# Routing per image with rows scattered to expert lists, and experts started on three images' full blocks while the last image is normed and routed

## The chip, the cores and the metric

The kernel runs on one core of a Trainium2 chip. The metric is the device time of one launch in microseconds (us). PE is TensorE, PEld its weight loads, DVE VectorE, ACT ScalarE, POOL GpSimd, SP SyncE, which here only issues DMAs. A name with a q behind it (SPq) is an engine's instruction queue.

## The reference

Four images of 256 channels x 1024 pixels go through group norm and a full attention over pixels, a second attention on layer-normed tokens, and a mixture of experts. The last part is what the change is about:

```
t = t + _L1_attn_ref(_ln_t(t), ...)
t = t + _L1_ffn_ref(_ln_t(t), ...)
# _L1_ffn_ref, 4096 tokens of 256 numbers, 8 experts, 1024 hidden units:
x_norm = _layernorm(x, ln_g, ln_b)
xf = x_norm.reshape(B * S, D)
probs = jax.nn.softmax(xf @ gate_w, axis=-1)
dispatch_w, expert_idx = jax.lax.top_k(probs, TOP_K)        # TOP_K = 2
combine = jnp.sum(jax.nn.one_hot(expert_idx, E) * dispatch_w[..., None], axis=1)
for e in range(E):
    h = jax.nn.gelu(xf @ w1[e] + b1[e], approximate=False)
    out = out + combine[:, e:e + 1] * (h @ w2[e] + b2[e])
return x + out
```

For the inputs of the reference, experts 0 to 7 are chosen 471, 363, 1370, 373, 1459, 939, 273 and 2944 times; in the first three images 371, 263, 1011, 276, 1133, 680, 215 and 2195 times.

## The kernel before, in words

Every float32 product is made of three passes (`three`) over a rounded half and a remainder of each operand; ACT makes the rounded half (a cast), DVE the remainder (a subtraction). All engines run hand-written programs that meet at semaphores.

**Images.** `image(b, first, last)` runs on each engine for b = 0 to 3. Its first part is the pixel attention, its second the group R of 24 projections (`for gi, ... in enumerate(R)`), its third the second attention: eight turns of `scores` and `mix2` on PE. The norms of image b-1, the transposes of its normed rows (`gate_turn`) and its gate products (`gate`, logits to `gate_read`) are woven into image b. Those of image 3 stand behind it, on their own. SP writes the stream (`acc_rows`) and the normed rows (`xf_rows`) of each image to memory.

**Routing.** After image 3 and after a meeting of all engines (`ends(..., 1, ...)`), `route` on DVE finds each token's two experts, its place in its expert's list, and with 64 matmuls on one-hot matrices (`pick_lo`, `pick_hi`) the tables `gather_at`, `scatter_at` and `slot_w`. Lists are padded to blocks of 256 rows.

**Expert steps.** A step s is one block of one expert; experts come in ascending order, and with the counts above there are 2, 2, 6, 2, 6, 4, 2 and 12 blocks, 36 steps. Steps run in pairs (i, n), s = 2i + n, in a loop. In a step, PE makes for f = 0 to 7 a first product (hidden columns 128f to 128f+127) and a second product, with first products three f ahead (`AHEAD = 3`), and at f = 1 it transposes the rows of step s+1 (`x_turn`). ACT makes the gelu of each first product into one of four slots `h32`, DVE splits it into `hs`; second product f waits for that (`h_lo`). At f = 3 ACT scales the output of step s-1 (`y_scale`, into `y_w`, semaphore `y_act`), and POOL adds it to the stream with two indirect DMAs (`scatter`, semaphore `added`). POOL also gathers the rows of step s+2 with two indirect DMAs (`gather`).

**Weights.** A step's raw weights (w1 and w2 of an expert, 1 MB each) are loaded by SP (`expert_load`) into buffer n = s mod 2, and split in eight pieces of 512 columns by ACT (`w_piece`) and DVE. Split weights have two buffers too (`w1s[n]`, `w2s[n]`), so step s compares its expert with that of step s-2 (`fresh`); if it is the same one, nothing is loaded or split. Here that makes 16 loads. The pieces of step s+1 are made during step s, at ACT's f = 0 to 7.

**End.** SP waits for the last scatter, loads the stream, PE transposes it, and SP stores the output.

Of the kernel before, what the change touches and what calls it, by code (L numbers as in the profile page):

```python
# [29 lines left out]
P = 128  # L30
ALU = mybir.AluOpType
# [19 lines left out]
def hybrid_block_kernel(nc, x, q_w, k_w, v_w, oT, q_b, v_b, out_b, gn, W1, W2T, a_qk, a_vT, Wout,  # L51
# [15 lines left out]
    COLS = STEPS * SUB  # L67
# [3 lines left out]
    assert KC == 2 and STEPS % 2 == 0 and NT == 8 and NH == 2 and TILES * E == 256  # L71
# [4 lines left out]
    xf_d = nc.dram_tensor("xf_rows", (TOK, C), F32, kind="Internal").ap()  # L76
    acc_t = acc_d.rearrange("(t p) c -> p t c", p=P)
    xf_t = xf_d.rearrange("(t p) c -> p t c", p=P)
# [4 lines left out]
    with ctx:  # L83
# [18 lines left out]
        logits = sb("logits", [P, TILES, E])  # L102
        top8 = sb("top8", [P, TILES, 8])
        top_i = sb("top_i", [P, TILES, 8], mybir.dt.uint32)
# [15 lines left out]
        bs("to_224", [P, 56])  # L120
        pr = [bs(f"pr{i}", [P, 2, T], F32R) for i in range(2)]
        bs("to_0", [P, 8])
        xf = bs("xf", [P, NT, C])
# [4 lines left out]
        xfT = sb("xfT", [P, KC, T], F32, here)  # L128
        here.close()
# [10 lines left out]
        x2 = sb("x2", [P, NT, C], F32, here)  # L140
# [7 lines left out]
        sb("to_32", [P, 8], F32, here)  # L148
# [4 lines left out]
        minus_one = bs("minus_one", [P, 8])  # L153
# [24 lines left out]

        tl_bn = bs("tl_bn", [P, 2, NT, 6])
        tl_mv = bs("tl_mv", [P, 2, NT, 2])  # L180
        tl_eps = bs("tl_eps", [P, 2, NT])
        tl_r = bs("tl_r", [P, 2, NT])
        tl_mr = bs("tl_mr", [P, 2, NT])
        tl_nb = bs("tl_nb", [P, 2, NT])
        batch_scope.close()


        route_scope = ExitStack()

        def rs(name, shape, dt=F32):  # L190
            return sb(name, shape, dt, route_scope)

        expert_of = ctx.enter_context(nc.sbuf_tensor("expert_of", [P, STEPS], I32))

        fresh = ctx.enter_context(nc.sbuf_tensor("fresh", [P, STEPS + 2], I32))
        live = sb("live", [P, PAIRS], I32)
        last_step = sb("last_step", [P, 1], I32)
        gather_at = sb("gather_at", [P, COLS + 2 * SUB], I32)
        scatter_at = sb("scatter_at", [P, COLS], I32)
        slot_w = sb("slot_w", [P, COLS])  # L200
        before = rs("before", [P, P])
        iota_i = rs("iota_i", [P, P], I32)
        iota = rs("iota", [P, P])
        top_f = rs("top_f", [P, 2, TILES])
        exps = rs("exps", [P, TILES, E])
        zsum = rs("zsum", [P, TILES])
        zinv = rs("zinv", [P, TILES])
        is_top = rs("is_top", [P, 2, TILES, E])
        either = rs("either", [P, TILES, E])
        scratch = rs("scratch", [P, 2, TILES, E])  # L210
        top_w = rs("top_w", [P, 2, TILES])
        prefix = [rs(f"prefix{i}", [P, TILES, E]) for i in range(2)]
        slot_all = rs("slot_all", [P, TILES, E])
        cnt_f = rs("cnt_f", [P, E])
        cnt_i = rs("cnt_i", [P, E], I32)
        cnt_s = rs("cnt_s", [P, E], I32)
        need = rs("need", [P, E])
        ends_t = [rs(f"ends{i}", [P, E]) for i in range(2)]
        base = rs("base", [P, E])
        past = rs("past", [P, STEPS, E])  # L220
        expert_f = rs("expert_f", [P, STEPS])
        other = rs("other", [P, STEPS])
        end_i = rs("end_i", [P, 1], I32)
        slot_f = rs("slot_f", [P, 2, TILES])
        slot_i = rs("slot_i", [P, 2, TILES], I32)
        lo_i = rs("lo_i", [P, 2, TILES], I32)
        hi_i = rs("hi_i", [P, 2, TILES], I32)
        lo_f = rs("lo_f", [P, 2, TILES])
        hi_f = rs("hi_f", [P, 2, TILES])
        number_i = rs("number_i", [P, TILES], I32)  # L230
        number = rs("number", [P, TILES])
        PICK = 8
        pick_lo = rs("pick_lo", [P, 2 * TILES, P])
        pick_hi = rs("pick_hi", [P, 2 * TILES, 2, COLS])
        one_hot = rs("one_hot", [P, 2 * TILES, COLS])
        at_f = rs("at_f", [P, COLS])
        at_m = rs("at_m", [P, COLS])
        route_scope.close()
# [7 lines left out]
        es("to_512", [P, 16])  # L246
        xg = es("xg", [P, 2, SUB, C])
        xt = [[es(f"xt{n}{i}", [P, KC, STEP], F32R) for i in range(2)] for n in range(2)]
        h32 = es("h32", [P, 4, STEP])
        hs = [es(f"hs{i}", [P, FC, STEP], F32R) for i in range(2)]  # L250
        y_b = es("y_b", [P, SUB, C])
        y_w = es("y_w", [P, 2, SUB, C])
        es("w1_to_32", [P, 8])
        w1s1 = [es(f"w1s1{i}", [P, KC, FF], F32R) for i in range(2)]
        es("w2_to_192", [P, 40])
        w2s1 = [es(f"w2s1{i}", [P, FC, C], F32R) for i in range(2)]

        es("past_route", [P, 10240])
# [3 lines left out]
        es("w1_to_224", [P, 8])  # L262
        w1s = ([es(f"w1s0{i}", [P, KC, FF], F32R) for i in range(2)], w1s1)
        es("w2_to_32", [P, 16])
# [180 lines left out]
        def _(sp):  # L445
# [98 lines left out]
            with sp.Fori(1, PAIRS) as i:  # L544
                with is_live(sp, i):
                    for n in range(2):
                        expert_load(i * 2 + n, n, i, False)
# [1411 lines left out]
```

## Time and profile before

| | us |
|---|---|
| Median of 3 runs (1246.24 to 1247.96) | 1247.34 |
| The profiled execution's own time | 1251.48 |
| Its span, first to last instruction | 1249.8 |
| PE busy in it | 1149.5 |
| End of the last `mix2` to the first expert product | 93.8 |
| First expert product to the end of the last one | 431.7 |

A row of the timeline gives start, duration, engine, line, operation, out<-in, count, and in brackets the idle time of the engine before it with what ended it. Rows of one engine that follow each other closely are merged, with their count. PE's rows overlap: a row's duration is longer than its distance to the next.

### The profile page before, as it was taken

The page shows a single profiled execution, that of the slowest core. Times are in us where ns is not written, and L with a number is a line of the kernel's source. Part 1 is how long each engine was busy: PE and PEld are TensorE (multiplying, and loading weights), DVE is VectorE, ACT ScalarE, POOL GpSimd, SP SyncE. Part 2 cuts the span into 40 slices and gives each one's busy share as a digit, 9 for nine tenths or more (in the row PEclk, how much of TensorE's full clock was granted, in tenths as well). Part 3 has the DMA queues.
Part 4 walks back from the last instruction along what each step waited for, and adds up shares of the span by engine and source line. Part 5 has one row for each costly group of instructions (what it writes and reads, how often), then busy time and mean ns, then how long its engine had stood idle before and what let it go on. Part 6 is the DMA issues. An engine that isn't in the chain of part 4 may idle for free.

```text
span 1249.8 us, 25051 instructions
## 1 busy us (share of the span) xinstructions
PE 1149.5 (92%) x8118; PEld 1072.8 (86%) x8119; DVE 823.7 (66%) x1883; ACT 545.2 (44%) x995; POOL 343.2 (27%) x352
## 2 busy tenths in 40 slices
PE   6999999999999999999999334999999999999993
PEld 5898998988988989989898234999999999999992
DVE  4676475964667744778436787796796778856651
ACT  2533445432435334444333313674564556634431
POOL 0010002500004300024000325355555455555440
PEclk9999999999999999999999558899999999999996
DMA  5000000210001100011000233363573547533238
GB/s 165 1 2 33 1 1 1 69 34 1 1 2 35 68 1 1 1 35 35 1 1 1 67 114 107 101 193 54 164 207 53 145 100 215 150 59 55 55 47 273
DMA packets 66206, 82.70 MB, mean 66 GB/s; under 512 B 11104, under 2 KB 56544, under 8 KB 66144
## 3 DMA queue, kind: packets, MB, share of 16 engines
q1 hardware_dynamic: 52128, 63.48, 15.8%
q0 software_dynamic: 14016, 18.37, 8.2%
q8 instruction: 42, 0.69, 0.2%
q14 instruction: 20, 0.16, 0.0%
HBM read 60.85 MB, written 22.02 MB: 66 GB/s over the span
## 4 chain that ended last, share of the span: by engine, by line
PE 89%; DVE 6%; DMA 2%; issue 1%; SPq 1%; ACT 1%; POOL 0%; POOLq 0%; DVEq 0%; ACTq 0%
PE ps L1553 81%; PE ps L1633 2%; PE ps L1843 1%; PE ps L1595 1%; PE ps L1566 1%; DMA rows<-acc_rows 1%; DVE one_hot L1103 1%; DVE pick_hi L1111 1%; PE ps L1586 1%; PE ps L1642 1%; PE ps L1655 1%; DVE pick_lo L1106 1%; DMA o_row<-in_out_b 1%; DMA xg<-xf_rows,now_g 0%; SPq L559 0%
## 5 line engine op out<-in xcount | busy, mean ns | idle before, releaser
L1553 PE MATMUL ps<-xt,w1s 128*128 128x256 f32 x1746 | 257.5, 284 | 1.5 <-DVE xt L1484 1.5
L1553 PE MATMUL ps<-w2s,hs 128*128 128x256 f32 x1728 | 250.1, 280 | 3.3 <-issue 2.5
L1553 PEld LDWEIGHTS ps<-xt,w1s 128*128 128x128 f32 x1746 | 227.9, 190 | 2.3 <-DVE xt L1484 1.9
L1553 PEld LDWEIGHTS ps<-w2s,hs 128*128 128x128 f32 x1728 | 222.8, 188 | 4.7 <-issue 4.7
L952 ACT ACTIVATE h<-ps,b1t 128x256 f32<-128x256 f32 x288 | 137.4, 478 | 112.4 <-PE ps L1553 78.8
L712 POOL DMA_INDIRECT acc_rows<-y_w,now_s x72 | 119.9, 1666 | 165.3 <-issue 154.2
L1520 DVE CAST hs<-h 128x256 fp32r<-128x256 f32 x288 | 92.1, 320 | 70.1 <-ACT h L952 48.2
L1522 DVE TENSOR_TENSOR hs<-h,hs 128x256 fp32r<-128x256 f32 x288 | 123.0, 427 | 9.9
L1553 PE MATMUL ps<-xs,wh 128*128 128x512 f32 x384 | 121.3, 397 | 1.5 <-issue 1.5
L594 POOL TENSOR_TENSOR tl_r<-tl_eps,minus_half 128x4 f32<-128x4 f32 x16 | 16.2, 1014 | 350.0 <-DVE tl_eps L1224 350.0
L699 POOL DMA_INDIRECT xg<-xf_rows,now_g x76 | 92.8, 1222 | 47.4 <-POOL now_g L695 34.7
L1553 PE MATMUL ps<-vs,pr 128*128 128x256 f32 x768 | 97.7, 283 | 0.0
L1553 PEld LDWEIGHTS ps<-vk,pr 128*128 128x128 f32 x768 | 92.4, 188 | 3.6 <-DVE pr L1365 0.9
L1553 PE MATMUL ps<-xs,qs 128*128 128x512 f32 x384 | 95.4, 397 | 0.0
L1553 PE MATMUL ps<-vk,pr 128*128 128x256 f32 x768 | 93.1, 277 | 0.7 <-DVE pr L1365 0.7
L1553 PE MATMUL ps<-qs,ks 128*128 128x512 f32 x384 | 93.2, 393 | 0.0
L1553 PEld LDWEIGHTS ps<-vs,pr 128*128 128x128 f32 x768 | 92.0, 188 | 0.0
L1360 DVE TENSOR_REDUCE neg_max<-ps 128x1 f32<-128x1024 f32 x32 | 39.2, 1224 | 79.9 <-PE ps L1553 79.9
L1553 PEld LDWEIGHTS ps<-qs,ks 128*128 128x128 f32 x384 | 70.2, 188 | 14.0
L1553 PEld LDWEIGHTS ps<-xs,wh 128*128 128x128 f32 x384 | 69.4, 188 | 14.5 <-issue 1.7
L1553 PEld LDWEIGHTS ps<-xs,qs 128*128 128x128 f32 x384 | 69.8, 188 | 13.5
L1553 PE MATMUL ps<-xs,wl 128*128 128x512 f32 x192 | 75.0, 391 | 0.0
(213 smaller groups left out, 1874.8 us busy)
## 6 DMA issues: line engine op xcount, KB each, us to landing
w1r<-in_w SPq DMA_DIRECT2D x16, 1024.0 KB
w2r<-in_w SPq DMA_DIRECT2D x16, 1024.0 KB, 8.6
b2t<-in_b SPq DMA_DIRECT2D x36, 128.0 KB
xn<-in_x SPq DMA_DIRECT2D x4, 1024.0 KB, 4.8
acc_rows<-r_out SPq DMA_DIRECT2D x4, 1024.0 KB, 4.5
xf_rows<-xf SPq DMA_DIRECT2D x4, 1024.0 KB, 5.0
rows<-acc_rows SPq DMA_DIRECT2D x8, 512.0 KB, 7.3
out_tokens<-cols_out SPq DMA_DIRECT2D x8, 512.0 KB, 8.8
```

The lines of the kernel that those rows point to most:

```text
L594: return g.tensor_tensor(dst, src, minus_half[:, 0:src.shape[1]], ALU.pow)
L699: g.indirect_dma_start(out=xg[:, n, h, :], out_offset=None, in_=xf_d, in_offset=bass.IndirectOffsetOnAxis(ap=now_g[:, n, h:h + 1], axis=0) ...
L712: g.indirect_dma_start(out=acc_d, out_offset=bass.IndirectOffsetOnAxis(ap=now_s[:, n, h:h + 1], axis=0), in_=y_w[:, n, h, :], in_offset=No ...
L952: a.activation(h32[:, gi % 4, :], bank(gi % 4, STEP), ACT.Gelu, bias=b1t[:, n, f:f + 1]).then_inc(h_act, 1)
L1103: v.tensor_tensor(one_hot[:, j, :], iota[:, 0:COLS].unsqueeze(1).to_broadcast((P, PICK, COLS)), hi_f[:, k, t].unsqueeze(2).to_broadcast((P ...
L1106: v.tensor_tensor(pick_lo[:, j, :], iota[:, :].unsqueeze(1).to_broadcast((P, PICK, P)), lo_f[:, k, t].unsqueeze(2).to_broadcast((P, PICK, P)),
L1111: v.tensor_tensor(pick_hi[:, j, 1, :], one_hot[:, j, :], top_w[:, k, t].unsqueeze(2).to_broadcast((P, PICK, COLS)), ALU.mult).then_inc(pic ...
L1360: v.tensor_reduce(neg_max[:, i:i + 1], bank(2 * (i % 2), count=2), AXX, ALU.max, negate=True).then_inc(s2_max, 1)
L1520: v.tensor_copy(hs[0][:, f, :], h32[:, gi % 4, :]).then_inc(h_hi, 1)
L1522: v.tensor_tensor(hs[1][:, f, :], h32[:, gi % 4, :], hs[0][:, f, :].bitcast(F32), ALU.subtract).then_inc(h_lo, 1)
L1553: ins = t.matmul(out, left[l], right[r], start=first and n == 0, stop=last and n == 2, **more)
L1633: ins = t.transpose(bank(4, count=2)[:, j * P:(j + 1) * P], prob[:, i % 2, j * P:(j + 1) * P], ident[:, :])
```

## The change

The routing of an image becomes part of the work woven into the next one. In group R, DVE takes logits to two experts per token (`gate_read`, `tops`, `choose`), PE sums how many earlier tokens chose the same expert (`ranks`, ten small matmuls), DVE makes list places and weights (`slots`, `weigh`), and POOL writes each normed row, with weights and row number behind its 256 numbers, to both of its experts' lists in memory (`send_rows`, 16 indirect DMAs an image). Lists have a fixed place for each expert. `x2`, the tables of one-hot matrices and `xf_rows` are gone.

When three images are in the lists, their full blocks are 1, 1, 3, 1, 4, 2, 0 and 8; the first 12 of them are steps 0 to 11 (phase A, experts in descending order), and the rest is phase B in ascending order. With the counts above the steps' experts are 5 5 4 4 4 4 3 2 2 2 1 0 | 0 1 2 2 2 3 4 4 5 5 6 6, and 7 twelve times. The norms, gate, routing and row writes of image 3 are placed by hand at certain (s, f) of steps 0 to 8 (`on`, `..._AT`). Steps 0 to 9 are written out; the loop begins at step 10, behind nine DMAs that write empty rows to the lists' ends, and behind the last row writes.

Split weights now have one buffer (`w1s`, `w2s`); `fresh` compares step s with step s-1, which makes 13 loads: for steps 0, 2, 6, 7, 10, 11, 13, 14, 17, 18, 20, 22 and 24. Six pieces are made during the step before, from ACT's f = 1 on (`W_AT`), two during the step itself (`LATE_AT`). The rows of a step are one plain DMA by SP; they bring the row numbers and weights, which POOL copies out before SP may fill the buffer again (`note_step`, semaphore `noted`).

```diff
+    A_STEPS = 12
+    B_STEPS = STEPS - A_STEPS
+    LOOP_AT = A_STEPS // 2 - 1
...
+        RANK_AT = 21
+        RANK_BANK = 3
+        EARLY = {4: (0, 1), 5: (2, 3), 6: (4, 5), 7: (6, 7)}
+        W_PIECES = ((0, 0), (0, 1), (1, 0), (0, 2), (1, 1), (0, 3))
+        W_AT = {1: 0, 3: 1, 4: 2, 5: 3, 6: 4, 7: 5}
+        LATE_AT = {0: 2, 3: 3}
...
+        STATS_AT = {(0, 1): 0, (0, 2): 1}
+        XF_AT = {(0, 4): (0,), (0, 5): (1,), (0, 6): (2,), (0, 7): (3,), (1, 0): (4,), (1, 1): (5,), (1, 2): (6,), (1, 4): (7,)}
+        GATE_TILES_AT = {(2, 4): (0, 1), (2, 5): (2, 3), (2, 6): (4, 5), (2, 7): (6, 7)}
+        ROWS_AT = {4: (0,), 5: (1, 2), 6: (3, 4), 7: (5, 6), 8: (7,)}
```

The loads on SP:

```diff
+            def gather(s, n, first):
+                if not first:
+                    sp.wait_ge(xt_mm, at(s, 1, -1))
+                    sp.sem_inc(sp_held, 1)
+                    sp.wait_ge(noted, at(s, 2, -2))
+                    sp.sem_inc(sp_held, 1)
+                row = sp.value_load(row_of[0:1, bass.ds(s, 1)], min_val=0, max_val=PAD)
+                sp.dma_start(xg[:, n, :, :], sorted_d[bass.ds(row, STEP), :].rearrange("(h p) c -> p h c", p=P)
+                             ).then_inc(g_in[n], 16)
...
+            def expert_load(s, n, u):
+
+                sp.wait_ge(wl_act, at(s, LATE, -LATE))
+                sp.sem_inc(sp_held, 1)
+                sp.wait_ge(wl_dve, at(s, LATE, -LATE))
+                sp.sem_inc(sp_held, 1)
+                e = expert(s)
+                with sp.If(sp.value_load(fresh[0:1, bass.ds(s, 1)], min_val=0, max_val=1) == 1):
+                    weights(n, e)
...
+            def steps(i, first):
+                for n in range(2):
+                    s = i * 2 + n
+                    if not first:
+                        expert_load(s, n, i)
+                    gather(s + 2, n, False)
+                    if isinstance(i, int) and s == 3:
+                        rows_of(B - 1)
...
+            for e in range(E + 1):
+                at_row = sp.value_load(pad_at[0:1, e:e + 1], min_val=0, max_val=PAD - STEP) if e < E else PAD
+                sp.dma_start(sorted_d[bass.ds(at_row, STEP), :].rearrange("(h p) c -> p h c", p=P),
+                             pad_row[:, :].unsqueeze(1).to_broadcast((P, SUB, ROW))).then_inc(pad_in, 16)
+            sp.wait_ge(pad_in, (E + 1) * 16)
+            sp.wait_ge(rows_in, B * NT * 2 * 16)
+            with sp.Fori(LOOP_AT, PAIRS) as i:
```

POOL:

```diff
+            def send_rows(b, tiles):
+
+                pool.wait_ge(slot_done, at(b, 1, 1))
+                pool.wait_ge(weighed, at(b, 1, 1))
+                pool.sem_inc(pool_held, 1)
+                for t in tiles:
+                    for k in range(2):
+                        g.indirect_dma_start(out=sorted_d, out_offset=bass.IndirectOffsetOnAxis(
+                            ap=slot_i[:, k, t:t + 1], axis=0), in_=xf[:, t, :], in_offset=None,
+                            bounds_check=PAD - 1, oob_is_err=True).then_inc(rows_in, 16)
...
+            def note_step(s, n, u):
+
+                if not (isinstance(s, int) and s < 2):
+                    pool.wait_ge(added, at(s, SUB * 16, -SUB * 16))
+                pool.wait_ge(g_in[n], at(u, 16, 16))
                 pool.sem_inc(pool_held, 1)
...
+                e = pool.value_load(expert_of[0:1, bass.ds(s, 1)], min_val=0, max_val=E - 1)
+                g.tensor_copy(now_s[:, n, :], xg[:, n, :, NUMBER]).then_inc(noted, 1)
+                g.tensor_copy(now_w[:, n, :].unsqueeze(2),
+                              xg[:, n, :, bass.ds(e + WEIGHT, 1)]).then_inc(noted, 1)
...
+            def steps(i):
                 for n in range(2):
                     s = i * 2 + n
...
+                    if not (isinstance(i, int) and s == 0):
+                        scatter(s - 1, 1 - n, isinstance(i, int) and s == 1)
+                    note_step(s + 1, 1 - n, (i if n == 0 else i + 1))
```

ACT (the gelu lines stand as before):

```diff
+            def w_piece(s, n, u, which, p):
+
+                first = isinstance(s, int) and s == 0
+                act.wait_ge((w1_in, w2_in)[which][n], at(u, 16, 16))
+                if not first:
+                    act.wait_ge((h_mm, y_mm)[which], at(s, FC, 2 * p + 2 - FC))
...
                     a.activation(h32[:, gi % 4, :], bank(gi % 4, STEP), ACT.Gelu,
                                  bias=b1t[:, n, f:f + 1]).then_inc(h_act, 1)
...
+                    if late and f in LATE_AT:
+                        w_piece(s, n, i, 1, LATE_AT[f])
+                    if split and f in W_AT:
+                        w_piece(s + 1, 1 - n, (i if n == 0 else i + 1), *W_PIECES[W_AT[f]])
```

PE:

```diff
+            def ranks(b, at_bank, c):
+
+                pe.wait_ge(chosen, at(b, 1, 1))
+                out = bank(at_bank)
+                t.matmul(out[:, c:c + NT * E], before[:, :], either[:, :, :].rearrange("p t e -> p (t e)"),
+                         start=True, stop=False)
+                for d in range(1, NT):
+                    t.matmul(out[:, c + d * E:c + NT * E], ones[:, :],
+                             either[:, 0:NT - d, :].rearrange("p t e -> p (t e)"), start=False, stop=False)
...
-            pe.wait_ge(p2_exp, B * NT)
-            gate_turn(B - 1)
-            gate(B - 1, range(NT))
-            pe.wait_ge(g_mm, B)
-            pe.sem_inc(pe_end, 1)
```

**The order on SP.** In the loop before, the rows from one weight load's first wait to its DMAs, in the odd step of a pair. They wait for the pieces of an earlier step alone.

```order
L513 ISA [waits ws_act,ws_dve]
L513 TENSOR_LOAD expert_of
L513 ISA x2
L524 REGISTER_ALU
L524 TENSOR_LOAD fresh
L524 ISA x2
L524 COMPARE_AND_BRANCH
L516 ISA
L516 DMA w1r<-in_w 128x2x1024
L518 DMA w2r<-in_w 128x8x256
```

Now, in the written-out steps, from the rows of step s+2 to the weights of step s+1.

```order
L541 TENSOR_LOAD row_of [waits xt_mm,noted]
L541 ISA x2
L542 ISA
L542 DMA xg<-sorted_rows 128x2x272
L546 TENSOR_LOAD expert_of [waits wl_act,wl_dve]
L546 ISA x2
L555 TENSOR_LOAD fresh
L555 ISA x2
L555 COMPARE_AND_BRANCH
L517 ISA
L517 DMA w1r<-in_w 128x2x1024
L519 DMA w2r<-in_w 128x8x256
```

The load of step s+1 now stands behind a wait for `noted` of step s.

**The order on POOL.** Now, one step in the written-out part: the scatter of step s-1, then the note of step s+1.

```order
L762 DMA acc_rows<-y_w,now_s 4096x256 [waits noted,y_act]
L762 DMA acc_rows<-y_w,now_s 4096x256
L751 TENSOR_LOAD expert_of [waits added,g_in0]
L751 ISA x2
L752 CAST now_s<-xg 128x2
L753 ISA
L753 COPY now_w<-xg 128x2
```

The note waits for `added`, which the two DMAs ahead of it raise when they have landed.

**The order on ACT.** Now, in the loop, the start of a step whose successor has new weights: the second gelu, the first weight piece, the third gelu.

```order
L1049 ACTIVATE h<-ps,b1t 128x256 [waits h_lo]
L965 ISA
L967 ISA [waits w1_in0]
L970 CAST w1s<-w1r 128x2x256 [waits h_mm]
L1046 REGISTER_ALU
L1048 REGISTER_ALU [waits h_mm]
L1049 ACTIVATE h<-ps,b1t 128x256 [waits h_lo]
```

The third gelu of step s stands behind the wait for w1 of step s+1. Before, the first piece stood one gelu earlier and waited for its load in the same way.

## Rows read from the trace of the kernel before

**Rows 1.** The page's busy time of each engine.

```profile
PE 1149.5 (92%) x8118; PEld 1072.8 (86%) x8119; DVE 823.7 (66%) x1883; ACT 545.2 (44%) x995; POOL 343.2 (27%) x352
```

**Rows 2.** PE's timeline from the last mix2 to the first expert products.

```profile
684.56 5.93 PE L1553 MATMUL ps<-vk,pr 128*128 128x256 f32 x48 [0.71 <-DVE pr L1365]
...
784.29 5.01 PE L1553 MATMUL ps<-xt,w1s 128*128 128x256 f32 x24 [1.46 <-DVE xt L1484]
```

**Rows 3.** Timeline of all engines at the last step's end.

```profile
1215.11 0.87 PE L1553 MATMUL ps<-w2s,hs 128*128 128x256 f32 x6
...
1220.64 1.55 POOL L712 DMA_INDIRECT acc_rows<-y_w,now_s  x1 [0.30 <-issue]
1223.74 7.14 SPq L559 DMA_DIRECT2D rows<-acc_rows  x8
```

**Rows 4.** The chain that ended last: seven steps without new weights lie between.

```profile
1112.54 11.25 PE ps L1553 x96
...
1194.43 11.28 PE ps L1553 x96
```

**Rows 5.** Timeline of all engines in one step with new weights.

```profile
811.42 0.48 ACT L952 ACTIVATE h<-ps,b1t 128x256 f32<-128x256 f32 x1 [0.42 <-PE ps L1553]
...
813.58 0.60 PE L1843 MATMUL ps<-ident,xg 128*128 128x128 f32 x4
...
815.58 0.92 ACT L967 ACTIVATE y_w<-y_b,slot_w 128x256 f32<-128x256 f32 x2
...
816.14 0.87 PE L1553 MATMUL ps<-w2s,hs 128*128 128x256 f32 x6
...
817.90 1.62 POOL L712 DMA_INDIRECT acc_rows<-y_w,now_s  x1 [4.23 <-issue]
...
819.83 1.91 POOL L712 DMA_INDIRECT acc_rows<-y_w,now_s  x1 [0.31 <-issue]
...
820.52 0.44 DVE L1522 TENSOR_TENSOR hs<-h,hs 128x256 fp32r<-128x256 f32 x1
...
820.88 0.68 DVE L1474 TENSOR_TENSOR w2s<-w2r,w2s 128x512 fp32r<-128x512 f32 x1
```

**Rows 6.** Timeline around two weight loads: SP's issues, and ACT's first piece.

```profile
910.99 0.35 SPq L540 DMA_DIRECT2D b2t<-in_b  x1
...
914.72 0.01 SPq L516 DMA_DIRECT2D w1r<-in_w  x1
...
919.59 0.62 ACT L912 CAST w1s<-w1r 128x512 fp32r<-128x512 f32 x1 [2.67 <-DMA w1r<-in_w]
...
922.99 0.34 SPq L540 DMA_DIRECT2D b2t<-in_b  x1
925.15 0.38 SPq L516 DMA_DIRECT2D w1r<-in_w  x1
...
930.24 0.62 ACT L912 CAST w1s<-w1r 128x512 fp32r<-128x512 f32 x1 [0.91 <-DMA w1r<-in_w]
```

**Rows 7.** Windows: stretch, its length, PE busy, granted clock (1.00 full, 0.50 half), DMA.

```profile
692.00:696.00 4.00, 0.00 (x0) 0.63 0.00 0
696.00:700.00 4.00, 0.00 (x0) 0.50 0.01 2
...
786.00:788.00 2.00, 2.00 (x11) 0.50 0.30 102
788.00:790.00 2.00, 2.00 (x17) 0.86 0.00 0
```

**Rows 8.** DVE's timeline in the gap: `tail_add` and `tail_stats` for four tiles of image 3.

```profile
690.60 1.29 DVE L1208 TENSOR_TENSOR tok<-ps,tok 128x512 f32<-128x512 f32 x2 [3.97 <-PE ps L1553]
691.92 1.41 DVE L1219 BATCH_NORM_STATS2 tl_bn<-tok 128x6 f32<-128x256 f32 x4
...
693.77 0.17 DVE L1224 TENSOR_SCALAR tl_eps<-tl_mv 128x4 f32<-128x4 f32 x1
```

**Rows 9.** Timeline of PE in group R of image 2: a quarter of the gate.

```profile
448.43 0.95 PE L1595 MATMUL ps<-gate_sb,xfT 128*128 128x8 f32 x8
```

More of the change, by code:

```diff
@@ L201, in hybrid_block_kernel @@
[L201 to L224, printed above, removed]
@@ L858, in image @@
                         hi2(0)
+                    if not first and gi == RG - 4:
+                        route_exp(b - 1)
                     if gi == TN_AT - 1:
@@ L949, in chunks @@
                     act.wait_ge(h_mm, at(i, 2 * FC, gi + 1))
-                    if not (first and gi < 4):
+                    if not (new and gi < 4):
                         act.wait_ge(h_lo, at(i, 2 * FC, gi - 3))
@@ L1318, in image @@
                         max1(i + 2)
+                    if not first and i == 0:
+                        tail_stats(b - 1, 1)
                     if i >= 1:
@@ L1322, in image @@
                         norm1(i - 2)
-                    if not first and i in DVE_TAIL:
-                        tail_stats(b - 1, *DVE_TAIL[i])
                     if i == 6:
@@ L1497, in _, with on @@
             x_lo(0, 0)
-            def steps(i, first):
+            tail_add(B - 1, 0)
+            def on(s, f):
+                if (s, f) == (0, 0):
+                    tail_add(B - 1, 1)
+                if (s, f) in STATS_AT:
+                    tail_stats(B - 1, STATS_AT[s, f])
+                for j in XF_AT.get((s, f), ()):
+                    tail_xf(B - 1, j)
+                if (s, f) == READ_AT:
+                    gate_read(B - 1, 7, 0)
+                if (s, f) in TOPS_AT:
+                    tops(TOPS_AT[s, f])
+                if (s, f) == CHOOSE_AT:
+                    choose(B - 1)
+                if (s, f) == SLOTS_AT:
+                    slots(B - 1, 7, 0)
+                if (s, f) == WEIGH_AT:
+                    weigh(B - 1)
+                if (s, f) in TABLE_AT:
+                    (table_b1, table_b2, table_b3)[TABLE_AT[s, f]]()
@@ L1517, in chunks @@
                     dve.wait_ge(h_act, at(i, 2 * FC, gi + 1))
-                    if not (first and n == 0):
+                    if not (new and n == 0):
                         dve.wait_ge(y_mm, at(i, 2 * FC, gi + 1 - FC))
@@ L1711, in image @@
                         gate(b - 1, GATE_MM[gi])
+                    if not first and gi == RANK_AT:
+                        ranks(b - 1, RANK_BANK, 0)
                     if not last and gi in PE_GN:
```

1179 lines of the change are left out of this document (650 added, 529 removed).

## The prediction

> **What bounds the kernel now.** I read the busy times first: PE is busy for 1149.5 of 1249.8 us [rows 1], so time can only come from the 100 us in which it is not, or from work taken off it. Then PE's timeline. The last `mix2` ends at 684.56 + 5.93 = 690.49, the first expert product starts at 784.29 [rows 2]: 93.8 us hold nothing but the last image's norms, gate and routing. The 36 steps after it run to 1215.98 [rows 3], 431.7 us. Seven steps without new weights take 1194.43 - 1112.54 = 81.89, 11.70 each [rows 4], and 36 of these would be 421.2; so loads, splits and a slow start cost 10.5 us now. Last the windows: after 690.49 the granted clock is 0.63 over 692 to 696 and 0.50 from 696 on; from 784.29 it stays 0.50 until about 788.6 (0.86 over 788 to 790) [rows 7]. PE falls to the lower level (1.2 GHz) some 2.5 us after it stops, and takes 4.3 us of products to come back.
>
> **What the change takes away.** The gap, -93.8. The 10.5 of the steps goes too, since I price all stalls of the new steps anew: -10.5.
>
> **What it adds in the images.** `ranks` is ten matmuls for each image. A quarter of the gate is four small matmuls (x8 in the record) in 0.8 us of PE [rows 9], so 0.2 each, 2.1 with the wider ones. `choose` is a chain of seven short DVE operations, of which one takes 0.17 [rows 8]; it starts when group R has two projections left, and I let PE wait 0.7 for it and 0.3 for `slots` and `weigh`: 3.1 x 3 images = 9.3. In the last image the tables, first weight pieces and `x_turn` add an estimated 2.6: +11.9. POOL's 16 row DMAs an image cost nothing: even at 1.91 + 0.31 each, like a scatter [rows 5], they take 36 us, and the eight turns of `mix2` that hide them take longer than that; beyond some 45 us the first gather would be late.
>
> **What it adds in the first steps.** DVE has, in steps 0 and 1, 16 splits of 0.70 (the subtraction alone 0.44) and 6 pieces of 0.68, 0.60 with their overlap [rows 5], `tail_add` 2 x 1.3 and `tail_stats` 2 x 2.0 [rows 8], 8 `tail_xf` of two dependent 256-column operations (2 x 0.44), and 1.8 of x and y work: 11.2 + 3.6 + 2.6 + 4.0 + 7.0 + 1.8 = 30.2. With some 4.5 of waits (first gelu, weights of step 2) it is 34.7 for what PE could do in 23.4: +11.3. Gate, transposes and ranks of image 3 now lie between products, about 6 on PE, and the tables on DVE another 1: +7.
>
> **What it adds at each change of expert.** This term decides. Take T for the start of the transposes in a step (PE's f = 1), 813.58 in [rows 5].
> - `y_w` ends at T + 2.9 (815.58 + 0.92). POOL's scatters start 1.4 later there; I take T + 4.0. From the first's start to the second's end is 3.8: T + 7.9.
> - It has landed by T + 9.1: at the end 1220.64 + 1.55 = 1222.19 is followed by SP's dependent load at 1223.74 [rows 3]; of these 1.55 I take 1.2.
> - POOL's note is a register load and two copies; no row shows it. Below it is nothing, above two copies like `now_g`, 1.5; I take 1.1, and `noted` comes at T + 10.2, which is 1.5 before the next step's T.
> - Only then may SP issue the rows of step s+2, and behind them look up and issue the weights of step s+1. In the odd step of a pair the two lookups take 925.15 - 923.33 = 1.8, in the even one, with the loop's end, 914.72 - 911.34 = 3.4 [rows 6]; the gather ahead takes about 1.1. Weights are issued at T + 1.4 or T + 3.0.
> - w1 reaches ACT 5.1 later (925.15 to 930.24), 4.9 in the other load [rows 6]: T + 6.5 or T + 8.1.
> - ACT waits for it before its third gelu. The second gelu, just before 811.42, ends at T - 3.2. Then piece (0.62), its remainder (0.6) and the split of the third gelu (0.7) take 2.1, and PE's second product f = 2, which would start at T + 2.6 (816.14), starts at T + 8.6 or T + 10.2. **PE stalls 6.0 or 7.5 us at a change of expert.**
>
> Before, the load waited only for a buffer, and ACT waited 0.9 and 2.7 for it [rows 6]; the row DMAs were POOL's own business.
>
> The 13 loads: step 0's is hidden, step 2's is in the first steps. Steps 6, 13 and 17 cost 6.0; steps 20, 22 and 24 (even, in the loop) 7.5; 7, 14 and 18 follow a change directly and find `noted` some 2 us earlier against T, since PE restarted slowly: 4.0, 5.5, 5.5. Together 18.0 + 22.5 + 15.0 = 55.5. Step 10's load stands behind nine writes of empty rows at about 0.95 (a lookup and an issue), their landing (2) and the loop's entry (3.4): 20.6 by the sum above with `noted` where it was, more since POOL's rows delay it, less for overlap; I take 21. Step 11's load follows at once, 0.5. Sum 77.
>
> PE stands idle for 4 us or more in ten of these stalls, longer than the 2.5 after which its clock was halved, and each restart then loses as at 784.29: 4.3 us at about half speed, where four groups took 5.01 instead of 2.8 [rows 2], so 1.85 each: +18.5.
> The rule that speaks against the change is in the Trainium skill, "TensorE: Matmul & The Clock Gate", "HAM oscillation — how this bites in real kernels": a loop that waits for its operand before each piece of work restarts cold each time. The rows agree with it; without it the sum is 18.5 lower.
>
> **Sum.** 1249.8 - 93.8 - 10.5 + 11.9 + 11.3 + 7 + 77 + 18.5 = 1271.2 us of span. The profiled execution took 1251.48 with a span of 1249.8, the median of three runs is 1247.34, 2.5 below that span: **1269 us**, 1.7% slower.
> For a landed scatter the Trainium skill, "DMA: Bandwidth & Descriptors", "Anatomy of one DMA — SWDGE (gpsimd) path", gives a fixed cost of about 2.0 us, most of it the write receipt; the trace has at most 1.55 behind POOL's span. An estimate by the page, with 2.0 for my 1.2, would put ten stalls 8 us higher in all.
>
> **Rivals.**
> - *Weights late, but less (17%).* If ACT's and DVE's work after the landing overlaps more, or `noted` comes 3 us earlier, a stall is 3 us, the clock stays up, and step 10 waits 12: 77 + 18.5 becomes 42, the span 1218, the median **1215**. For it: POOL's spans are rough and the note has no row. Against: all links but the note have rows. Here the change is faster; the sign turns when stalls and restarts together fall below 74.
> - *Weights in time (5%).* Only step 10's wait is left, about 10: 1186, median **1183**. It needs SP to issue 8 us earlier than the order on SP allows.
> - *More (6%).* Nested branches on ACT and DVE and ten written-out steps make instruction fetch wait, or the lists' row DMAs slow DVE: 1 us more on each of 36 steps, **1305**. Against: the seven light steps of [rows 4] lose nothing to their branches now.
> - *The routing in the images is the cost (2%).* If every operation there lay on PE's path, 12 us an image, and the stalls were as above: 1300.
>
> **How the numbers follow.** The stalls as summed have 70%, by themselves 1250 to 1292: a step's stall 4.5 to 7.5 for ten (15 either way), restarts 10 to 22, step 10's wait 15 to 27. The range over the cases is 1228 to 1296; it leaves out the lower half of the first rival, the second, and part of the last two. Faster by over 0.2% (about what such a measurement can tell from no change): the first two rivals, 22%. Slower: 75%. Within: 3%.
>
> **What the changed profile would show.** Right: no gap behind the last `mix2`; ACT's waits led by w1r's DMA, 9 to 11 us at nine switches; PE idle before a second product by 4 to 8 us, once by 21 before step 10, with the clock at 0.5 behind each; SP waiting for `noted` before each gather; steps 0 and 1 at 17 us each with DVE nearly full. Wrong: w1r issued more than a step ahead, PE's stalls under 3 us, or a clock of 1.00 through the steps.

## The result, and the profile after

The changed kernel takes **1411.5 us** (median, 1411.08 to 1414.55), 1.130 times the time before (95% interval 1.128 to 1.132). The forecast was 1269 in a range of 1228 to 1296: the sign is right, the size is not, by some 140 us. The profiled execution has a span of 1409.0 us against 1249.8.

The page's first row and its instruction queue q14, and q14 in the page of before, which [rows 1] don't show (packets, MB, share of 16 engines):

```profile
PE 1192.7 (85%) x8066; PEld 1106.6 (79%) x8067; DVE 761.6 (54%) x1859; ACT 522.6 (37%) x938; POOL 278.3 (20%) x319
...
q14 instruction: 189, 1.55, 0.4%
```
```profile
q14 instruction: 20, 0.16, 0.0%
```

PE is busy 43 us longer than in [rows 1] for slightly less work: that is clock (a mean of 0.924 against 0.963). And nearly ten times as many bytes of code come over q14; the experiments below tie these packets to ACT and DVE. I divide the expert steps by the transposes: **turn k** reaches from the transposes of step k's rows to those of step k+1's. In turn k the weights of step k arrive and are split, so "step k costs" in the forecast is turn k here. Windows of the changed kernel (stretch, length, PE busy, granted clock, DMA): turns 0 to 5, 6 to 25, 26 to 35, and the rest.

```profile
727.73:813.99 86.26, 76.01 (x629) 0.96 0.32 73
813.99:1208.10 394.11, 276.20 (x2003) 0.84 0.40 105
1208.10:1361.94 153.84, 125.83 (x1003) 0.89 0.27 45
1361.94:1408.95 47.01, 21.00 (x154) 0.75 0.61 194
```

The same cuts for all profiles on which this document rests (us; the columns add up to the span):

| | images, to turn 0 | turns 0-5 | turns 6-25 | turns 26-35 | rest |
|---|---|---|---|---|---|
| before | 781.7 | 68.5 | 238.3 | 117.0 | 44.2 |
| changed kernel | 727.7 | 86.3 | 394.1 | 153.8 | 47.0 |
| e9, one more instruction | 699.7 | 83.8 | 394.6 | 153.6 | 46.6 |
| e1, weights first | 699.7 | 82.4 | 348.1 | 156.0 | 46.5 |
| e2, two copies of the code | 699.7 | 83.0 | 354.9 | 118.6 | 43.9 |
| e3, both | 699.5 | 81.5 | 279.1 | 118.4 | 45.5 |
| e8, and empty rows early | 699.8 | 81.5 | 272.4 | 118.4 | 45.2 |
| e7, e3 with spread row DMAs | 703.9 | 84.2 | 281.1 | 118.5 | 45.5 |
| e6, spread row DMAs | 702.1 | 84.7 | 393.7 | 156.9 | 46.5 |
| e11, two copies on DVE alone | 730.3 | 83.9 | 366.2 | 139.5 | 43.6 |
| e5, before with a branch | 782.1 | 71.4 | 249.6 | 117.6 | 44.2 |
| e10, before with a long loop | 781.7 | 80.8 | 317.1 | 150.8 | 46.0 |

The last ten turns are the ones to start from. They are light (no new weights), and before they took 11.70 each, as in [rows 4]; now the even ones take 17.1 to 18.7 and the odd ones 12.3 to 13.0. The change has nothing there that SP or a DMA could be late with for PE. The waits of the changed kernel (engine and line <- released by: us in all, times, longest):

```profile
PE ps L1730 <- DVE hs L1694: 147.0, 35, 18.5
ACT w1s L970 <- DMA w1r<-in_w: 124.9, 12, 21.9
POOL now_s L752 <- DMA acc_rows<-y_w,now_s: 111.0, 34, 4.3
DVE hs L1692 <- DVEq L1677: 95.7, 15, 9.3
ACT h L1049 <- ACTq L1034: 77.3, 19, 6.2
```

The w1r row is the forecast's stall. The two rows with a q are the engines' own queues, and L1677 and L1034 are the last instructions before the step's code where the next step has no new weights (`no_pieces`). DVE at such a place, turn 32, in the timeline:

```profile
1305.94 0.38 DVE L1692 CAST hs<-h 128x256 fp32r<-128x256 f32 x1 [0.64 <-ACT h L1049]
1306.36 0.43 DVE L1694 TENSOR_TENSOR hs<-h,hs 128x256 fp32r<-128x256 f32 x1
1315.99 0.29 DVE L1692 CAST hs<-h 128x256 fp32r<-128x256 f32 x1 [9.21 <-DVEq L1677]
```

What its queue did in those 9.2 us (the two last numbers of times are first and last start). L1710 is the loop's end, L452 the branch on `live`, L1658 and L1668 the branches on `fresh`, L1676 what follows the second:

```profile
L1710 DVEq COMPARE_BRANCH  x1: 56/56/56, 1306.4 to 1306.4; - x1
L1710 DVEq FUSED_REGOPS  x1: 63/63/63, 1309.7 to 1309.7; - x1
...
L452 DVEq COMPARE_BRANCH  x1: 55/55/55, 1310.4 to 1310.4; - x1
...
L1643 DVEq FUSED_REGOPS  x4: 64/127/190, 1312.3 to 1313.9; - x4
...
L1658 DVEq COMPARE_BRANCH  x1: 63/63/63, 1313.0 to 1313.0; - x1
...
L1680 DVEq ALU_OP  x1: 45/45/45, 1313.2 to 1313.2; - x1
...
L1668 DVEq COMPARE_BRANCH  x1: 56/56/56, 1314.1 to 1314.1; - x1
...
L1676 DVEq FUSED_REGOPS  x1: 53/53/53, 1315.6 to 1315.6; - x1
```

Three times nothing is done: 3.3 us behind the jump back (1306.4 to 1309.7); 1.8 in straight code up to the load of `fresh` (behind 1310.4), where DVE also waits for the step's biases, but their last semaphore update is at 1306.7, so it isn't them; and 1.5 behind the jump over one variant (1314.1 to 1315.6). The jump over two variants before it (1313.0 to 1313.2, L1658 to L1680) costs nothing: a jump alone isn't dear. In the kernel before the same jump back is followed at once:

```profile
L1533 DVEq COMPARE_BRANCH  x1: 56/56/56, 1165.5 to 1165.5; - x1
L1533 DVEq FUSED_REGOPS  x1: 62/62/62, 1165.8 to 1165.8; - x1
```

### The profile page after: what moved, and what is told of

The parts are those of the page before. It is cut to its first block and busy times, and to the rows that moved or that the text cites. A ratio compares the mean times of both kernels' runs of the same rounds, so it can differ in the third digit from the quotient of the medians.

```text
span 1409.0 us, 25384 instructions
## 1 busy us (share of the span) xinstructions
PE 1192.7 (85%) x8066; PEld 1106.6 (79%) x8067; DVE 761.6 (54%) x1859; ACT 522.6 (37%) x938; POOL 278.3 (20%) x319
## 5 line engine op out<-in xcount | busy, mean ns | idle before, releaser
L1730 PE MATMUL ps<-w2s,hs 128*128 128x256 f32 x1728 | 275.7, 298 | 147.7 <-DVE hs L1694 147.0
L1730 PEld LDWEIGHTS ps<-w2s,hs 128*128 128x128 f32 x1728 | 244.5, 206 | 155.9 <-issue 78.3
L1730 PE MATMUL ps<-xt,w1s 128*128 128x256 f32 x1746 | 274.3, 296 | 0.5 <-issue 0.5
L1730 PEld LDWEIGHTS ps<-xt,w1s 128*128 128x128 f32 x1746 | 244.3, 204 | 0.4 <-issue 0.2
L1692 DVE CAST hs<-h 128x256 fp32r<-128x256 f32 x288 | 85.9, 298 | 194.5 <-DVEq L1677 95.7
L1730 PE MATMUL ps<-qs,ks 128*128 128x512 f32 x384 | 98.9, 402 | 9.6 <-issue 8.8
L1730 PE MATMUL ps<-vk,pr 128*128 128x256 f32 x768 | 99.0, 285 | 7.5 <-issue 5.0
L1572 DVE TENSOR_TENSOR w1s<-w1r,w1s 128x512 fp32r<-128x512 f32 x52 | 35.6, 687 | 88.6 <-ACT w1s L970 88.6
L686 POOL DMA_INDIRECT sorted_rows<-xf,slot_i x64 | 65.0, 1016 | 87.7 <-DVE xf L1267 58.8
L970 ACT CAST w1s<-w1r 128x512 fp32r<-128x512 f32 x52 | 32.1, 621 | 124.9 <-DMA w1r<-in_w 124.9
```

What stands on the lines that cost most here:

```text
L686: g.indirect_dma_start(out=sorted_d, out_offset=bass.IndirectOffsetOnAxis(ap=slot_i[:, k, t:t + 1], axis=0), in_=xf[:, t, :], in_offset=No ...
L970: a.copy(halves[0], raw_of(n)).then_inc(wl_act if late else ws_act, 1)
L1572: v.tensor_tensor(halves[1], raw_of(n), halves[0].bitcast(F32), ALU.subtract).then_inc(wl_dve if late else ws_dve, 1)
L1692: v.tensor_copy(hs[0][:, f, :], h32[:, gi % 4, :]).then_inc(h_hi, 1)
L1730: ins = t.matmul(out, left[l], right[r], start=first and n == 0, stop=last and n == 2, **more)
```

## The experiments

Two theories at the start. **Weights late**: the forecast's stall, larger than summed. **Instructions late**: `chunks` now stands four times in the loop (`late` x `split`), so that the body no longer stays in the engine. The bodies as built have 191 instructions on ACT and 228 on DVE before, 385 and 435 in the changed kernel; these counts, and those below, take in the 17 to 19 instructions that stand directly behind the loop. (The expectations of e2 and e4 count listed rows, which merge equal neighbours and leave plain waits out.)

**e1: weights first.** SP's order in a step:

```diff
-                    if not first:
-                        expert_load(s, n, i)
+                    if not (first and n == 0):
+                        load_weights(s + 1, 1 - n, (i if n == 0 else i + 1))
                     gather(s + 2, n, False)
+                    if not (first and n == 0):
+                        load_biases(s + 1, 1 - n)
```

> SP issues the weights of step s+1 ahead of the rows of step s+2, no longer behind `noted`; the biases follow the rows; nothing else differs from the changed kernel. Weights-late theory (the forecast's): the stalls of PE at a change of expert in steps 6, 7, 10, 11 and 13 to 24 go, step 10's with them, about 64 us of stalls and 10 of clock, and the even steps without weights become 11.7 again: about 1270 or less. Instruction theory: the stalls that are not the weights' stay, since ACT and DVE still wait for their own code at each pass of the loop; the five even steps without weights at the end stay near 18.1 us, the even steps with weights keep 5 to 6 us of stall, and the time is about 1340.

**e2: two copies.** On ACT and DVE (shown for ACT):

```diff
-                    with act.If(fresh_at(s)):
-                        with act.If(fresh_at(s + 1)):
-                            chunks(i, n, True, True)
...
+                    late = None if isinstance(i, int) and s == 0 else fresh_of(s)
+                    with act.If(fresh_of(s + 1) == 1):
+                        chunks(i, n, late, True)
+                    with act.Else():
+                        no_pieces(s)
+                        chunks(i, n, late, False)
...
-                    if late and f in LATE_AT:
-                        w_piece(s, n, i, 1, LATE_AT[f])
+                    if late is not None and f in LATE_AT:
+                        with act.If(late == 1):
+                            w_piece(s, n, i, 1, LATE_AT[f])
```

> ACT's and DVE's step code stands twice and not four times (with and without the pieces of the next expert); the late pieces of an expert stand under small branches inside it, with the same work in the same places. DVE's loop body falls from 393 listed rows to about 230, ACT's from 293 to about 180 (197 and 143 in the kernel before). Instruction theory (the body no longer stays where the engine holds its instructions, so each pass fetches it anew): the even steps of the last ten fall from 18.1 to 12 or 13 us, the stalls in the looped steps with new weights fall by 3 to 8 each, in all 60 to 80: about 1340. Branch theory (it is the register loads and branches themselves that cost, not their fetch): there are as many or more of them, so nothing is gained: 1405 to 1420. Weights-late theory: no change, since SP is untouched.

**e3: both.**

> Both edits at once. If the two causes add, about 1411 - 71 - 75 = 1265, and less if each alone leaves stalls that the other hides (down to 1225: the steps then begin at 728 and take 11.7 each plus some 20 in the first, and the end takes 47). If one of the theories is empty this run equals the other's.

Measured: e1 **1333.0** (ratio to before 1.067, interval 1.064 to 1.069), e2 **1300.8** (1.041; 1.038 to 1.043), e3 **1226.7** (0.983; 0.980 to 0.986). Both theories hold, and e3 is faster than the kernel before. But 28 us of each gain have nothing to do with the edit: all three reach turn 0 at 699.5 to 699.7, the changed kernel at 727.7. With them put back e1 would be at 1361, e2 at 1329 and e3 at 1255, so e1 fell short of both theories' figures. I come to the 28 us under e9, which has the changed kernel's steps without them and takes 1380.5; against it e1 gains 47.5, e2 79.7 and e3 153.8.

In e2 the last ten turns are as before: its windows of turns 6 to 25 and 26 to 35, and DVE's wait at a pass of the loop:

```profile
782.63:1137.54 354.91, 263.51 (x2003) 0.85 0.44 114
1137.54:1256.17 118.63, 117.58 (x1003) 1.00 0.33 57
```
```profile
1195.34 0.29 DVE L1670 CAST hs<-h 128x256 fp32r<-128x256 f32 x1 [3.37 <-DVEq L1656]
```

There are more branches in it than in the changed kernel (16 compares in the body, as built, against 8), and the wait falls from 9.2 to 3.4 us: the branches were cheap, the fetch behind them was not. Its q14 has 41 packets. In e1 those ten turns stay at 156.0, as the instruction theory had it.

e3 gains 27 us more than e1 and e2 together. Turns 12 and 13 show why: together 31.8 us in e9, 36.1 in e1, 31.9 in e2, 24.5 in e3. With the code fetched in turn 12, SP had time to bring turn 13's weights; with the code in place the weights were what was waited for. Turns 16 and 17 go the same way (30.7, 33.3, 32.5, 23.8). Each cause stood in for the other there. So the price of one depends on whether the other is left: the code costs 80 us with the weights late (e9 to e2) and 106 with the weights in time (e1 to e3), the order on SP 47 (e9 to e1) or 74 (e2 to e3).

**e5 and e4: does a branch, or a third copy, cost anything in the kernel before?** Control and test, on ACT and DVE:

```diff
+                    if not first:
+                        with act.If(act.value_load(live[0:1, bass.ds(i, 1)], min_val=0, max_val=1) == 0):
+                            act.sem_inc(act_end, 1)            # e5
+                            chunks(i, n, first, True)          # e4, in its place
```

The control, e5:

> Control of the run with the third copy: the same extra load and never-taken branch in each looped step on ACT and DVE, with one instruction behind it instead of a copy of the step. The engines get one more register load and a jump per step, about 0.8 us of their queues; a step without splits has idle time for it and a step with them may not: 1249 to 1265.

And e4:

> The kernel before, with one more branch in each looped step on ACT and DVE that is never taken, and behind it a third copy of the step's code: DVE's loop body grows from 197 to 306 listed rows, ACT's from 143 to 223, no work is added. Instruction theory: the body no longer stays in the engine and each of the 18 passes fetches anew, 3 to 6 us a pass: 1249 + 55 to 110 = 1300 to 1360, and the instruction queue q14 goes from 20 packets to well over 100. Branch theory: the same as its control with the short branch, 1249 to 1265. If the body that still fits lies above 306 rows, there is no difference to the control either.

Measured: e5 **1261.6** (1.008; 1.006 to 1.010), e4 **1263.9** (1.011; 1.009 to 1.012). The branch costs 0.3 us a step, mostly in steps that split weights; light turns take 11.7 to 11.9 in both. The third copy costs about 2 us: bodies of 285 (ACT) and 350 (DVE) still stay in the engines, with 22 packets on q14. That left the theory open, since the body was not yet as long as the changed kernel's.

**e10: as long as the changed kernel's.** In place of the copy, 91 plain copies on ACT and 98 on DVE in each step, which are never executed:

```diff
+                            for copy in range(91):
+                                a.copy(h32[:, 0, :], h32[:, 1, :])
```

> The kernel before with the never-taken branch of its control (1261.6 us) and behind it 91 plain copies on ACT and 98 on DVE in each looped step, never executed: the loop body has 383 and 434 instructions, the sizes of the changed kernel's (385 and 435), where the third copy of the step had left it at 285 and 350 without a cost. Instruction theory: each pass now fetches its code anew on both engines; light even steps go from 11.8 to 16 or more, q14 from 20 packets to above 100, and the time is 1261.6 + 18 passes of 3 to 6 us = 1315 to 1370. If the length of the body isn't what counts, it is 1262 again.

Measured: **1377.2** (1.101; 1.098 to 1.105), 115.6 over its control, above the upper end of what was expected. Not an operation more is executed than in e5. Its windows of turns 6 to 25 and 26 to 35, DVE's and ACT's largest waits for their own queues, and its q14:

```profile
862.45:1179.58 317.13, 259.07 (x2002) 0.89 0.41 107
1179.58:1330.42 150.84, 129.98 (x1003) 0.91 0.27 45
```
```profile
DVE hs L1528 <- DVEq L1517: 87.3, 16, 7.0
ACT h L956 <- ACTq L945: 34.0, 18, 2.7
```
```profile
q14 instruction: 105, 0.86, 0.2%
```

The last ten turns take 150.8, like the 153.8 of the changed kernel: idle PE and, behind it, the lower clock (0.91). Code that is never executed does it. But only on DVE, which isn't what was expected. The same rows in e5, with the short bodies:

```profile
DVE hs L1526 <- DVEq L1515: 43.8, 19, 3.0
ACT h L955 <- ACTq L944: 34.1, 18, 2.7
```

ACT's row is the same in both, and in e10 its jump back is followed in 0.1 to 0.2 us at every pass, while DVE stands 2.7 to 3.4 us behind its own in 11 of the 17. So the body of 434 on DVE alone costs the 115.6 us, and ACT's 383 stay in the engine. In the changed kernel ACT does stand, 2.9 to 4.1 us behind the jump back in all 13 passes, with a body of 385. Two instructions more are not likely to be the reason; 182 of e10's are jumped over, 91 at a time, and where a body begins may count too. That was not tested. The Trainium skill, "Runtime: NRT & Kernel Launch", "Instruction fetch mechanics", says it in words: fetch runs ahead only in sequence, and a taken branch to code that isn't held waits for a DMA. The runs agree. It also gives the store of such an engine as 512 instructions in two halves; 435 didn't stay in it. The runs put the edge between 350 and 434 on DVE; on ACT 383 stayed in one kernel and 385 didn't in another.

**e11: DVE's half of e2.**

> Of the run with two copies of the step's code only DVE's half: DVE's loop body has 272 instructions, ACT's stays at 385. SP as in the changed kernel. At a light pass of the changed kernel ACT stands for 5.6 to 6.1 us between its last gelu and the next, DVE for 9.3 between its last split and the next. If DVE's own fetch sets PE's stall, a light even step is 13 to 15 us instead of 18.1 (ACT's share is left) and the time is 1300.8 (both halves) + 10 to 35 = 1310 to 1335. If ACT's fetch is what is waited for, the light even steps stay at 17 to 18 and the time is 1360 or more (1380 is the changed kernel without the 28 us in its images).

Measured: **1362.7** (1.089; 1.087 to 1.092), with the images' extra time back (turn 0 at 730.3). Without these 30.6 it is 1332, in the range given if DVE's fetch is what PE waits for. Light even turns are 14.0 to 15.8: 15.0 on average where the changed kernel has 18.1 and e2 12.1, so about half of the excess was DVE's; the rest is ACT's, whose wait for its queue is the changed kernel's:

```profile
ACT h L1050 <- ACTq L1035: 78.8, 21, 6.7
```

**e9, c0 and e6: the 28 us in the images.** Beside POOL's row DMAs (308.67 to 329.9 in image 1), PE's `scores` falls apart in the changed kernel, with no semaphore that it waits for (PE's timeline, the changed kernel first); in e9 it doesn't, though POOL's DMAs stand at the same place (308.49 to 330.8):

```profile
325.89 0.99 PE L1730 MATMUL ps<-qs,ks 128*128 128x512 f32 x3 [0.44 <-ACT prob L910]
327.69 0.39 PE L1730 MATMUL ps<-qs,ks 128*128 128x512 f32 x1 [0.81 <-issue]
328.41 1.11 PE L1730 MATMUL ps<-qs,ks 128*128 128x512 f32 x3 [0.33 <-issue]
330.52 1.01 PE L1730 MATMUL ps<-qs,ks 128*128 128x512 f32 x2 [1.01 <-issue]
331.96 1.64 PE L1730 MATMUL ps<-qs,ks 128*128 128x512 f32 x3 [0.43 <-issue]
```
```profile
325.10 2.89 PE L1731 MATMUL ps<-qs,ks 128*128 128x512 f32 x12
```

e6 spreads POOL's DMAs over the turns of `mix2`:

```diff
+                    if turn is not None:
+                        pool.wait_ge(s2_max, at(turn, NT, t + 1))
+                        pool.sem_inc(pool_held, 1)
```

> In images 1 to 3 POOL sends the two row DMAs of a tile after the DVE's maximum of the same turn of the second attention, not all sixteen in one burst; the number of DMAs and bytes is the same. Burst theory: PE's own gaps and slow turns of 4 to 10 us that stand beside the bursts (325 to 332, 497 to 510, 683 to 690) go, the first expert transposes come at 705 to 710 and not at 727.7, and the time is about 1390. If the gaps come from the number of row DMAs and not from their bunching, they are spread too and the time stays within 5 us of 1411.

Measured **1386.5** (1.110; 1.108 to 1.113), about what the burst theory gives. By itself it is no evidence for it: e1 and e2, taken on the same chip, leave the bursts alone and are rid of the same 28 us. So c0, the changed kernel with nothing edited:

> The changed kernel as it is. In its first profile the expert transposes start at 727.7 us; in four kernels whose images are the same line for line, or nearly so, they start at 699.5 to 699.7. If the 28 us belong to this program (where its code or buffers happen to lie), it takes about 1411 again with the same gaps at 325 to 332, 497 to 510 and 683 to 690; if they belonged to the chip or the session of that measurement, it takes about 1383 and the gaps are gone. The first is a little likelier, since four executions agreed within 3.5 us.

And e9, with one instruction more:

```diff
+            sp.sem_inc(sp_held, 1)
             ends(sp, 1, (pe_end, act_end, dve_end))
```

> The changed kernel with one more semaphore increment on SP, behind the last expert step; nothing waits for it. The 28 us that PE loses in the images of the changed kernel (twice measured) were gone in five kernels that differ from it only in the code of other engines or in later code. If they hang on where the program's code lies, this may move them too: 1383 with the expert transposes at 700; if it takes more of a change than one instruction, 1408 to 1412 again. No theory of the work itself would move the time here.

c0 took **1408.4** (1.126; 1.123 to 1.129) with the gaps, e9 **1380.5** (1.105; 1.103 to 1.107) without. It looks as if one instruction on SP, long behind the images, were worth 28 us. But the two were taken on different chips, and the record's chip numbers leave a rival standing:

| chip | row DMAs in bursts | row DMAs spread |
|---|---|---|
| 5 | gaps: c0, e11 | no gaps: e7 |
| 4 | no gaps: e1, e2, e3 | no gaps: e6 |
| 2 | no gaps: e8, e9 | |

The gaps may hang on the program (where its code or buffers lie) or on the chip: on chip 5 every kernel with bursts has them and the one with spread DMAs does not. The first run of the changed kernel has no chip on record, and neither c0 on chip 2 or 4 nor e9 on chip 5 was run. So the cause stays open, and the 28 us are not shown to belong to the change or to the instruction. PE's granted clock falls behind the gaps (0.98 up to 699.75 in the changed kernel, 1.00 in e9), which is part of the 28. Against e9, e6 is 6 us slower: its turn 0 starts 2.4 later, since PE waits 2.9 us for its first rows, and takes 1.5 longer.

**e8 and e7: the best version.** In e3 turns 10 and 11 still take 17.9 and 25.2. SP there:

```profile
843.65 9.99 SPq L601 DMA_DIRECT2D sorted_rows<-pad_row  x9
859.13 0.40 SPq L518 DMA_DIRECT2D w1r<-in_w  x1
```

e8 is e3 with these nine writes after step 7 (`if i == 3:` in the written-out steps) and not after step 9; their landing is waited for where it was.

> The run with weights first and two copies, and the nine writes of empty rows moved from the end of step 9 to the end of step 7 on SP (the waits for their landing stay where they were). In that run SP is held by them from 843.7 to 853.6 us, step 11's weights go out at 859.1, and steps 10 and 11 take 17.9 and 25.2 us. If the writes are what makes these weights late, the two steps take 12 to 14 each and the time is 1226.7 - 12 to 18 = 1209 to 1215. If it is the landing of the last rows or the loop's entry that holds SP, the gain is under 4 us: 1223 or more.

Measured: **1219.0** (0.976; 0.974 to 0.977), 7.7 less: turn 11 falls to 16.5, turn 10 stays at 18.5. By the order on SP the landing of the last rows and the loop's entry are what is left there; they were not tested apart. Half the expected gain. e7 is e3 with e6's spread:

> Weights first, two copies of the step code and row DMAs spread over the turns, all at once. The run with the first two took 1226.7, and its images lost nothing to the bursts. So if the spread matters only where PE's gaps stand, this run is the same, 1222 to 1230; if the bursts cost anything in that state too, it is up to 5 us faster.

**1232.8** (0.985; 0.984 to 0.987): 6 us worse than e3, outside what was expected, and the same 6 us as e6 against e9.

## Why the forecast was wrong in size

**The step that failed** is a term that the sum doesn't have. The forecast put the cost of the longer code at nothing. Only the rival "More (6%)" named it, instruction fetch behind nested branches and written-out steps, and priced it at 1 us for each of 36 steps. The ground against it was "the seven light steps of [rows 4] lose nothing to their branches now". That row is true and says nothing about the change: in the kernel before all of the loop stays in the engine, so its branches show the price of a branch, not of a fetch. The change doubles the body. What I should have set beside the row is the length of both bodies. The longer code costs 78.2 us of span (e9 to e2), more than twice the rival's 36, and 35 of them in ten turns that the forecast had at 11.7.

**The 28 us in the images** had no term. I know of no row of before that could have given them, and can't explain them now. With them gone the images are as summed: first expert product at about 703 in e2, against 690.49 + 11.9 = 702.4.

**The weights' stalls** were right in mechanism and nearly in size, which only e2 shows, where no fetch lies over them. Turn 20 of e2, all engines:

```profile
1029.30 1.55 POOL L763 DMA_INDIRECT acc_rows<-y_w,now_s  x1 [0.30 <-issue]
1032.89 0.42 POOL L753 CAST now_s<-xg 128x2 int32<-128x2 f32 x1 [2.04 <-DMA acc_rows<-y_w,now_s]
```
```profile
1035.06 0.60 PE L1974 MATMUL ps<-ident,xg 128*128 128x128 f32 x4
...
1037.65 0.39 SPq L518 DMA_DIRECT2D w1r<-in_w  x1
...
1042.77 0.62 ACT L971 CAST w1s<-w1r 128x512 fp32r<-128x512 f32 x1 [10.46 <-DMA w1r<-in_w]
...
1044.90 1.64 PE L1709 MATMUL ps<-w2s,hs 128*128 128x256 f32 x6 [7.14 <-DVE hs L1672]
```

The first two rows show POOL's scatter of the turn before and its wait before the note. From T = 1035.06: weights issued at T + 2.6 (forecast 3.0), ACT's piece at T + 7.7 (8.1), PE again at T + 9.8 (10.2), a stall of 7.1 (7.5; its terms give 7.6). The others, forecast in brackets: turn 6 5.2 (6.0), 7 5.9 (4.0), 10 22.0 (21), 11 5.4 (0.5), 13 6.9 (6.0), 14 7.7 (5.5), 17 5.7 (6.0), 18 6.4 (5.5), 22 7.9 and 24 7.7 (7.5). Together 88 against 77. Ten of these 11 us are in the turns that follow a change directly (7, 11, 14, 18): I gave them credit for a slow PE before them, and the chain through `noted` is slow too. The 20.6 of step 10 is a time from T, a stall of 18; the 21 that I took came close because `noted` came at T + 1.2 there and not at T - 1.5.

The links ahead of `noted` came out right in sum, in part by luck. POOL's wait of 2.04 us in the rows above is not all landing. Its queue goes on at 1032.0, 1.2 us behind the scatter's end, as I took it; then come the note's register load and its checks, 0.9:

```profile
L750 POOLq FUSED_REGOPS  x1: 43/43/43, 1032.0 to 1032.0; - x1
...
L752 POOLq TENSOR_LOAD <-expert_of x1: 292/292/292, 1032.3 to 1032.3; - x1
```

But 1.2 is the shortest landing in e2; on average it is 2.2 behind the scatter's end (2.8 at most). The Trainium skill, "DMA: Bandwidth & Descriptors", "Anatomy of one DMA — SWDGE (gpsimd) path", has about 2.0 us of fixed cost for such a DMA, most of it the write receipt; the average behind POOL's span is near it. What the landing took more, the scatters gave back by ending at T + 7.4 or sooner where I had 7.9, so `noted` was at T + 10.0 to 10.9 in turns 13, 20, 22 and 24 (10.2 forecast).

**Clock restarts**: in turns 6 to 25 of e2 PE is busy 263.5 us for work of 234, so 29.5 against 18.5. I had ten restarts at 1.85; there are eleven, at 2.7. The rows that I cited gave 5.01 - 2.8 = 2.2, not 1.85.

**First steps**: from the first expert product to turn 6, e2 takes 79.6 us. The forecast is 66.0 as before, less the 6.2 of the 10.5 that lie here, plus 11.3 and 7: 78.1. **The end and the gap** went as said; the gap behind the last `mix2` is gone.

In all, the forecast span of 1271.2 and 29 more is e2's 1300.1: 11 in the stalls, 11 in the restarts, 1.5 in the first steps, 3.5 in the rest of turns 6 to 25, 1.6 in the last ten, under 1 in the images and at the end. Then + 78 for the code, + 28 in the images and + 3 by which the first turns differ between two executions (86.3 and 83.8) make 1409. The sign was not luck: "Slower" had its 75% from the weights alone, and e2 bears that out: with the code in place and the 28 us gone, but the weights late, the ratio is 1.041. Of the rivals, "weights late, but less" and "weights in time" are refused by these stalls, and e3 shows that the order on SP was what kept the weights late: without it PE stalls by 4 us or more only once, 9.7 in turn 11. With the two repaired, the change does bring what it takes away: e8 is 2.4% faster than the kernel before.

## What to carry to other kernels

When a change makes variants of a loop's body, count the instructions of the whole body on each engine, before and after: a loop that stays in the engine and one that doesn't differ by some 7 us a pass here (115.6 over 17 in e10), and no operation shows it; the engine's queue does. A branch inside one copy of the code costs some 0.3 us a step; a copy too many can cost a fetch at each pass. And put on a queue first what has the longest way to its user: one order on SP was worth 47 to 74 us here.

Compare versions of a kernel by stretches as well as by totals, and on one chip. All four kernels of my first round were some 26 to 28 us faster than the changed kernel in a stretch that three of them don't touch. Without the cut by turns I would have put that down to the edits.

## What the runs showed of the hardware

- Bodies of 285 and 383 instructions (ACT) and 350 (DVE) were run without a fetch at each pass. A body of 434 on DVE cost 115.6 us over 17 looped pairs (e10 against e5), with nothing more executed, and 85 more packets of 8 KB. One of 385 on ACT stood 2.9 to 4.1 us behind each jump back in the changed kernel.
- In one pass of the changed kernel DVE stood 3.3 us behind the jump back, 1.8 in straight code and 1.5 behind a forward jump; another forward jump in the same pass cost 0.15.
- A scatter that adds rows landed 1.2 to 2.8 us behind POOL's span in e2, 2.2 on average. The idle time before POOL's note (3.3 on average, 4.3 at most in the changed kernel: 111.0 us, 34 times) holds 0.9 of register load and checks besides.
- PE stood and slowed beside bursts of indirect DMAs in some runs, 28 to 31 us in all, and not in others with the same work; chip and program were not separated.
